# Talking-heads attention in a 12-layer decoder kernel: a third score buffer, another block order, and other places for the maxima

## The reference, cut to what matters

```python
dots = jnp.einsum('bhid,bhjd->bhij', q, k) * QK_SCALE
dots = jnp.einsum('hg,bgij->bhij', W_pre_th, dots)
dots = jnp.where(causal[None, None], mask_value, dots)     # column > row is masked
top = jax.lax.top_k(dots, TOPK)[0]                         # TOPK = 64
dots = jnp.where(dots < top[..., -1:], mask_value, dots)
attn = jax.nn.softmax(dots, axis=-1)
attn = jnp.einsum('hg,bgij->bhij', W_post_th, attn)
out = jnp.einsum('bhij,bhjd->bhid', attn, v) * head_scale_params
out = out.transpose(0, 2, 1, 3).reshape(b, n, H * DH) * jax.nn.sigmoid(x @ Wg + bg)
return out @ Wo                                            # then residual and layer norm
```

## Time and profile before

| what | us |
|---|---|
| median of 3 executions (lowest, highest) | 1305.36 (1302.91, 1308.99) |
| the profiled execution: its own time | 1304.4 |
| the span of its instructions | 1302.6 |
| DVE busy in the span | 969.4 (74%) |
| PE busy | 892.4 (69%) |
| ACT busy | 640.1 (49%) |

### The profile page before, as it was taken

How to read it: one execution, slowest core, us unless ns; L and a number is a source line. 1 busy time by engine, 2 the same in 40 slices (tenths; PEclk the granted TensorE clock), 3 DMA queues, 4 the chain that set the end, 5 groups by cost and what they waited for, 6 DMA issues and landing times. The chain is left out here.

```text
span 1302.6 us, 18521 instructions
## 1 busy us (share of the span) xinstructions
PE 892.4 (69%) x6150; PEld 590.5 (45%) x6150; DVE 969.4 (74%) x2494; ACT 640.1 (49%) x1416; POOL 245.0 (19%) x369
## 2 busy tenths in 40 slices
PE   5957676565875304245997939889978615999876
PEld 3533334333544203134884514667645304666644
DVE  5899999937663798987356855888868497898832
ACT  3767878712442405046315713787447411666632
POOL 1330000001000000000012220299522022332100
PEclk9985555566997657577998968899979767999978
DMA  6000000002456001011100000000000000000000
GB/s 213 2 2 0 1 1 1 1 1 97 106 125 133 5 1 67 1 67 34 34 1 1 2 1 1 1 1 1 2 1 1 1 0 0 2 2 2 2 1 17
DMA packets 26607, 30.12 MB, mean 23 GB/s; under 512 B 1169, under 2 KB 23057, under 8 KB 25490
## 3 DMA queue, kind: packets, MB, share of 16 engines
q1 hardware_dynamic: 26514, 28.95, 8.0%
HBM read 19.50 MB, written 9.44 MB: 22 GB/s over the span
## 5 line engine op out<-in xcount | busy, mean ns | idle before, releaser
L1986 PEld LDWEIGHTS l2a_b_ps<-l2a_diag,l2a_uT 128*128 128x128 f32 x512 | 66.1, 197 | 27.9 <-issue 15.4
L1986 PE MATMUL l2a_b_ps<-l2a_diag,l2a_uT 128*128 128x128 f32 x512 | 70.6, 283 | 4.7 <-DVE l2a_convh L2197 3.7
L2683 PE MATMUL l1w_mem_ps<-l1a_rows,l1w_post 128*128 128x64 f32 x16 | 4.6, 381 | 96.5 <-DVE l1a_rows L2825 96.5
L2798 DVE MATCH_REPLACE8 l1w_minus<-l1w_low,l1w_minus 128x129 f32<-128x129 f32 (+39 forms) x264 | 65.2, 298 | 0.0
L2711 ACT ACTIVATE l1w_score<-l1w_mix_ps 128x264 f32<-128x264 f32 (+7 forms) x29 | 12.1, 451 | 107.4 <-DVE l1a_rows L2825 91.4
L2792 DVE MAX8 l1w_low<-l1w_minus 128x8 f32<-128x129 f32 (+37 forms) x332 | 60.4, 291 | 0.4
L2673 PE MATMUL l1w_mix_ps<-l1a_rows,l1w_pre 128*128 128x264 f32 (+7 forms) x58 | 29.4, 677 | 43.0 <-DMA l1a_rows<-scores_dram 25.4
L2656 POOL TENSOR_SCALAR_AFFINE_SELECT l1w_score<-l1w_score 128x256 f32<-128x256 f32 x8 | 4.1, 506 | 246.7 <-ACT l1w_score L2711 246.7
L2683 PEld LDWEIGHTS l1w_mem_ps<-l1a_rows,l1w_post 128*128 128x128 f32 x16 | 4.0, 288 | 100.8 <-DVE l1a_rows L2825 99.7
L613 ACT ACTIVATE l3a_l3x_probT<-l3a_l3x_turn_ps 128x512 f32<-128x512 f32 x64 | 38.2, 596 | 22.7 <-PE l3a_l3x_turn_ps L494 21.9
L494 PE MATMUL l3a_l3x_turn_ps<-pack,l3a_l3x_prob 128*128 128x128 f32 x256 | 40.7, 282 | 10.3 <-ACT l3a_l3x_probT L613 5.7
(11 more groups left out here) (580 smaller groups left out, 2822.7 us busy)
## 6 DMA issues: line engine op xcount, KB each, us to landing
scores_dram<-l1p_dots SPq DMA_DIRECT2D x8, 924.0 KB, 7.1
l1a_rows<-scores_dram SPq DMA_DIRECT2D x5, 1056.0 KB, 5.0
l1a_rows<-scores_dram SPq DMA_DIRECT2D x24, 132.0 KB, 3.6
scores_dram<-l1p_dots SPq DMA_DIRECT2D x8, 132.0 KB, 3.7
pack<-in_pack SPq DMA_DIRECT2D x1, 761.5 KB, 9.7
pack<-in_pack SPq DMA_DIRECT2D x2, 321.5 KB, 6.6
pack<-in_pack SPq DMA_DIRECT2D x1, 612.0 KB, 11.6
pack<-in_pack SPq DMA_DIRECT2D x1, 576.0 KB, 10.6
```

The source lines that it names most:

```text
L1986: mm = nc.tensor.matmul(bx_ps(n)[:, j * S:(j + 1) * S], uT[:, c, b, :], diag[:, s % 2, b, :], start=True, stop=True)
L2798: nc.vector.match_replace(out=neg[:, i, 0:keys[i]], in_to_replace=low[:, i, :], in_values=neg[:, i, 0:keys[i]], imm_value=LOWEST).then_inc ...
```

## The change

- `ORDER_K` is 7, 0, 6, 1, 5, 4, 3, 2.
- There are three score areas: `score_a` for blocks k=7, 5, 3, `score_b` for 6 and 4, and `cm.taps` for 0, 1, 2. `copy_mixed` waits only for the last block that was in the same area (`held_last`). `low` lies behind the scores in `cm.taps`, and `neg_max` and `total` have three places.
- TensorE and ScalarE work two blocks ahead: `mix(n+2)` behind `mix_again(n-1)`, `copy_mixed(n+2)` behind `copy_again(n-1)`.
- The maxima stand in other places (`MAX_AFTER`): of the second block after round 0 of the first; of n=3 after round 2 of n=2; of n=5 after round 2 of n=4; of n=6 after round 0 of n=5; of n=7 after the weights of n=5; of n=2 and n=4 at the start of the unsearched block ahead of them, as before.
- In the first block the negation and the searches of round 0 are done per half block, as soon as that half's scores are copied, and `maximum(0)` follows them. GpSimd's mask of the first block waits for both negations.
- As `cm.taps` is now used in the weights stage, the taps are loaded at the start of `mixed_output`, and `dve_weigh` stands in VectorE's stream there, in the turn b = 4.

```diff
-ORDER_K = (7, 0, 6, 1, 5, 2, 4, 3)
+ORDER_K = (7, 0, 6, 1, 5, 4, 3, 2)
+MAX_AFTER = {(0, 0): 1, (2, 2): 3, (4, 2): 5, (5, 0): 6}
...
-                sp.dma_start(cm.taps, cm.A["l2a_taps"]).then_inc(cm.taps_loaded, 16)
...
-                tap_weights.dve_weigh(nc, dve, cm)
...
+        held = {7: score_a[:], 5: score_a[:], 3: score_a[:], 6: score_b[:], 4: score_b[:], 0: cm.taps, 1: cm.taps, 2: cm.taps}
+        score = [held[k] for k in ORDER_K]
+        held_last = {1: 0, 2: 1, 5: 7, 4: 6, 3: 5}
...
                     pool.wait_ge(mix_set, filled[n + 1])
+                    if n == 0:
+                        pool.wait_ge(minus_set, 2)
...
                 mix(0)
+                mix(1)
                 for n in range(BLOCKS_K + 1):
-                    if n + 1 < BLOCKS_K:
-                        mix(n + 1)
                     if n:
                         mix_again(n - 1)
+                    if n + 2 < BLOCKS_K:
+                        mix(n + 2)
...
                 def copy_mixed(n):
-                    if n >= 2:
-                        act.wait_ge(weights_set, n - 1)
+                    if k in held_last:
+                        act.wait_ge(weights_set, ORDER_K.index(held_last[k]) + 1)
...
                 copy_mixed(0)
+                copy_mixed(1)
                 for n in range(BLOCKS_K + 1):
                     if n < BLOCKS_K:
                         exponentials(n)
-                    if n + 1 < BLOCKS_K:
-                        copy_mixed(n + 1)
                     if n:
                         copy_again(n - 1)
+                    if n + 2 < BLOCKS_K:
+                        copy_mixed(n + 2)
...
-                maximum(0)
                 for n, k in enumerate(ORDER_K):
...
+                        def negate(first, last):
+                            nc.vector.tensor_scalar(neg[:, first:last, :], s[:, first:last, :], -1.0, None,
+                                                    ALU.mult).then_inc(minus_set, 1)
+                        if n:
+                            dve.wait_ge(kth, n_kth)
+                            negate(cut[0], ROWS_K)
...
                             for i in cut:
+                                if n == 0 and r == 0 and i % (ROWS_K // 2) == 0:
+                                    dve.wait_ge(mix_set, filled[1] * (i + ROWS_K // 2) // ROWS_K)
+                                    negate(i, i + ROWS_K // 2)
+                                    n_minus += 1
+                                    dve.wait_ge(minus_set, n_minus)
...
+                            if n == 0 and r == 0:
+                                maximum(0)
...
-                            if r == 0 and n + 1 < BLOCKS_K:
-                                maximum(n + 1)
+                            if (n, r) in MAX_AFTER:
+                                maximum(MAX_AFTER[n, r])
...
                     nc.vector.tensor_tensor(e, e,
+                                            bcast_last(total[:, n % 3, :], w), ALU.mult).then_inc(weights_set, 1)
+                    if n == 5:
+                        maximum(7)
...
 def mixed_output(nc, cm, mixed, v_all, ahead):
+            def _(sp):
+                sp.dma_start(cm.taps, cm.A["l2a_taps"]).then_inc(cm.taps_loaded, 16)
...
                         bias(b + 1)
+                    if b == B // 2:
+                        tap_weights.dve_weigh(nc, dve, cm)
```

More of the change, by code:

```diff
@@ L2602, in mixed_weights @@
         pre, post = sc.sb("pre", [128, 128]), sc.sb("post", [128, 128])
-        score = [sc.sb(f"score{odd}", [128, ROWS_K * max(block_width(k) for k in ORDER_K[odd::2])])
-                 for odd in range(2)]
+        score_a, score_b = (sc.sb(n, [128, ROWS_K * block_width(k)]) for n, k in (("score_a", 7), ("score_b", 6)))
+        held = {7: score_a[:], 5: score_a[:], 3: score_a[:], 6: score_b[:], 4: score_b[:], 0: cm.taps, 1: cm.taps, 2: cm.taps}
+        score = [held[k] for k in ORDER_K]
+        held_last = {1: 0, 2: 1, 5: 7, 4: 6, 3: 5}
         blocks, loaded_rows, rows_count = ahead.blocks, ahead.loaded_rows, ahead.rows_count
         minus = sc.sb("minus", [128, ROWS_K * J])
-        low = sc.sb("low", [128, ROWS_K, 8])
-        neg_max, total = sc.sb("neg_max", [128, 2, ROWS_K]), sc.sb("total", [128, 2, ROWS_K])
+        low = cm.taps[:, ROWS_K * block_width(2):ROWS_K * block_width(2) + ROWS_K * 8].rearrange("p (i e) -> p i e", e=8)
+        neg_max, total = sc.sb("neg_max", [128, 3, ROWS_K]), sc.sb("total", [128, 3, ROWS_K])
         mem_w = sc.sb("mem_w", [128, MEM, S])
@@ L2654, in _ @@
                     pool.wait_ge(mix_set, filled[n + 1])
-                    part = block_of(score[n % 2], k)[:, :, w - ROWS_K:]
+                    if n == 0:
+                        pool.wait_ge(minus_set, 2)
+                    part = block_of(score[n], k)[:, :, w - ROWS_K:]
                     pool.affine_select(out=part, in_=part, compare_op=ALU.is_ge, fill=LOWEST, base=0,
@@ L2710, in copy_mixed @@
                         act.wait_ge(mix_mm, u + 1)
-                        nc.scalar.activation(score[n % 2][:, f * m * w:(f + 1) * m * w], mix_ps[u % 4][:, 0:m * w],
+                        nc.scalar.activation(score[n][:, f * m * w:(f + 1) * m * w], mix_ps[u % 4][:, 0:m * w],
                                              ACT.Copy).then_inc(mix_set, 1)
@@ L2718, in exponentials @@
                     w = block_width(k)
-                    s, e = block_of(score[n % 2], k), blocks[n % ROW_BUFS][:, :, 0:w]
+                    s, e = block_of(score[n], k), blocks[n % ROW_BUFS][:, :, 0:w]
                     for i in range(ROWS_K):
-                        last = nc.scalar.activation(e[:, i, :], s[:, i, :], ACT.Exp, bias=neg_max[:, n % 2, i:i + 1],
-                                                    accum_out=total[:, n % 2, i:i + 1])
+                        last = nc.scalar.activation(e[:, i, :], s[:, i, :], ACT.Exp, bias=neg_max[:, n % 3, i:i + 1],
+                                                    accum_out=total[:, n % 3, i:i + 1])
                     last.then_inc(exp_set, 1)
@@ L2836, in mixed_output @@
         ln = LayerNorm(sc)
+        tap_weights = TapWeights(sc)
         wg, wo, mem_v, mem_w = ahead.wg, ahead.wo, ahead.mem_v, ahead.mem_w
@@ L2843, in mixed_output @@
         with nc.Block() as block:
+            @block.sync
+            def _(sp):
+                sp.dma_start(cm.taps, cm.A["l2a_taps"]).then_inc(cm.taps_loaded, 16)
             @block.gpsimd
```

29 lines of the change are left out of this document (11 added, 18 removed).

## The result

The changed kernel took 1298.23 us, median of 6 executions (1296.81 to 1300.70), against 1304.07 (1302.90 to 1308.99, 6 executions) of the kernel before on the same chip. The medians differ by 5.8 us. The ratio that is given with a run is not the quotient of the two medians. Here it is 0.9945, interval [0.9924, 0.9965]: 7.2 us faster, between 4.6 and 9.9. The prediction was 1299.9. Of the twelve executions when the changed kernel ran for the third time, one took 2125.20 us; it counts as disturbed and is left out of the ratios.

The account below looks back on a forecast made before the run. No engine is full over the whole span; the weights stage decides, with a VectorE part and a 7.0 us TensorE/ScalarE tail. Profiled 1304.4 less 5.5 is 1298.9, plus 1.0 for the median gives 1299.9; range 1295.5 to 1305.

Parts of the forecast that it names:

- The start: First block of the weights stage: VectorE's searches begin at 428.2, first strike-out at 435.2 instead of 438.0; gain 2.7 us.
- The middle: Weights stage up to block k=5: waits ahead of maxima go, weights of k=5 at 576.7, 11.5 us earlier.
- What is late next: Stage's end, last load (k=2) held behind ScalarE's exponentials: three new waits, some 6 of 11.5 us gained go back.
- The tail: Copies-out ending the weights stage: last copy at 620.4, before 625.80, gain 5.4 us; output stage's products start 5.5 earlier.
- The taps: Scores stage gain 0 (at most 0.3 us); output stage: 1.23 us of weighing hidden, load's cost taken as 0.
- Warm tail: Rival, stage's end: TensorE's groups at the high clock (0.9) from 584; gain 8 us, median 1297.3; chance 0.20.
- Tail takes all back: Rival, stage's end: TensorE's groups stay at 1.7 us; gain 0.6 us, median 1304.8; chance 0.12.
- Taps in the way: Rival, output stage's start: taps' load holds up `mem_w` by up to 6.5 us; at full price 1306.4; chance 0.06.
- A wait stays: Rival, middle: a maximum still waits for a late load, each wait giving back 1 to 3 us; 1302; chance 0.07.

## Why the prediction was right

*The start.* Predicted: searches from 428.2, 435.2 at the first strike-out, gain 2.7. The trace: work from 427.98, and the maximum with its negation done at 432.52 + 2.33 + 0.17, that is 435.0. Its copies were 0.2 ahead, so this is what was forecast. Undoing it cost 3.5 us in time and 1.8 to 3.2 in the stage's length. Shown.

*The middle.* Predicted: no wait ahead of five maxima, and the weights of k=5 at 576.7. They were done at 576.07, without a wait. Of what makes this so, the third area (without it 10.7 us slower) and the later places of the maxima (without them 10.0 to 11.4 us more stage) are both needed in the two-ahead order, where both were tried. The prediction put the area's worth into the waits ahead of the maxima of k=6 and k=5, about 5 us; taking the area away cost twice that in the changed order, because the same wait also holds exponentials. With the area neither wait exists, so this does not show in the sum.

*Two blocks ahead* had no term of its own in the prediction, and rightly: one ahead was no slower.

*What is late next.* Predicted waits of 4.8, 2.3 and 6 to 7 ahead of the last three steps of VectorE; the trace has 4.00, 2.39 and 7.36. Predicted mechanism: ScalarE's exponentials hold the copies-out, these hold TensorE at its second PSUM bank and the last load. The experiment with the exponentials moved took away 4.00 and 2.39 and 5 of the 7.36 us, and the one with more banks took TensorE's wait for a bank there from 3.59 to 1.08. So of 12.1 us gained by 576 some 6 went back in the queue order of one engine; two edits, which together made the stage 10 to 12 us shorter, show it.

*The tail.* Last copy predicted at 620.4, found at 620.21; first product of the output stage 623.4, found 623.20. That these agree to 0.2 us is partly luck. Up to the last block the trace runs ahead of the forecast: the weights of k=5 are 0.6 early, TensorE ends their remixing at 584.45 + 3.06 = 587.51, not 588.6, and the load is there at 592.39, not 593.9, which is 1.5 early. Then the copies-out take it back. That of k=4 took 606.27 - 601.34 = 4.9 and that of k=3 615.99 - 611.30 = 4.7, not the 4.0 that I had put down for each as a mean of both clocks: their last groups came 1.71 us apart, the low clock's pace. These two terms were 1.6 too small together, and the terms ahead of them about as much too large.

The prediction took the low pace of the groups of k=5 from the rest of 4 to 5 us ahead of them. The pace was so, but the clock had not fallen in that rest, as the last section shows.

*The taps.* Predicted at nothing, hidden; the trace agrees for the scores stage (a wait of 1.56 in place of 0.32 and the 1.23 of work), for the weighing in the output stage (0.96 of waiting left of 2.23) and for the load beside `mem_w` (a wait of 0.66, before 0.80). This rests on the trace of the changed kernel and was not undone by an experiment.

*The rivals.* Warm tail: fell, as the groups of the three copies-out ran for the most part at the low clock. Its own terms, 1.6 and twice 0.8, lead to 617.2 and not to its 617.7, but nothing hangs on this. Tail takes all back: fell, since the last block's groups ran at the high clock. Taps in the way: fell. A wait stays: fell. The predicted 1299.9 is 1.7 us above the measured median. Of this, 1.3 lies in its starting point: it took 5.5 us off the 1305.36 of three executions, and all six have a median of 1304.07. The stage's gain was as forecast: 5.4 us in the profile of the result, 6.1 and 4.7 in the two later ones. The ratios say some 7 us for the whole kernel; whether the difference to 5.5 is more than the spread of whole executions stays open.

## What to carry to other kernels

When a buffer is added so that one engine doesn't wait, look next at the order inside the in-order queue of the engine that serves it: here half of the gain went back because a copy that had to wait stood ahead of exponentials that were ready, and these, done late, stood ahead of copies that free PSUM banks and a row buffer. Turning that queue's last entries round gave 5.6 us, beside the 7.7 of the whole change in the same set of runs, and cost no memory. A wait that is removed can come back at the next place: in the two-ahead order the third area without later places for the maxima made the kernel slower than before. A wait in front of an instruction is paid by all that is queued behind it: price it by them, not by its own user.

## What was not expected of the hardware

TensorE's clock changed several times near the end of the stage, and not when the engine's work stopped or began. These are windows of the changed kernel: three rests of TensorE, each followed by the groups behind it, and the last block's groups. The columns are length, busy us of TensorE, its weight loads, VectorE, ScalarE, GpSimd, then granted clock, DMA share, GB/s. A granted clock of 0.50 is 1.2 GHz, 1.00 is 2.4 GHz.

```profile
580.20:584.40 4.20, 0.00 (x0) 0.00 (x0) 4.17 (x27) 4.20 (x25) 0.00 (x0) 1.00 0.00 0
585.50:587.50 2.00, 2.00 (x10) 1.71 (x9) 1.93 (x14) 0.60 (x1) 0.00 (x0) 0.50 0.00 0
597.70:602.00 4.30, 0.00 (x0) 0.00 (x0) 1.74 (x13) 4.30 (x26) 0.00 (x0) 1.00 0.00 0
602.50:605.50 3.00, 3.00 (x16) 3.00 (x16) 1.53 (x2) 0.60 (x1) 0.00 (x0) 0.50 0.00 0
607.80:612.00 4.20, 0.00 (x0) 0.00 (x0) 0.54 (x2) 4.20 (x26) 0.00 (x0) 1.00 0.00 0
613.00:615.50 2.50, 2.50 (x14) 2.50 (x13) 0.00 (x0) 0.71 (x2) 0.00 (x0) 0.50 0.00 0
616.00:620.00 4.00, 3.57 (x31) 3.38 (x30) 0.00 (x0) 2.28 (x5) 0.00 (x0) 1.00 0.49 148
```

In all three rests the granted clock stayed at 1.00, and it fell to 0.50 only after TensorE had begun again, within 1 us. So most of the two groups behind each rest ran at the low clock, 1.7 us from the one to the other, and the last block's groups came 0.9 apart. In a longer rest of the kernel before, the 8.2 us from 606.9 to 615.1, the clock did fall within the rest: it was 1.00 until 609 and 0.50 from 609.5 on.

The version with early exponentials and more banks shows a fourth case. There TensorE's last run of groups began at 593.32 behind a rest of 2.63 us, and the clock was 0.50 from 586 on, before and in that rest; it stayed at 0.50 until 598 and was 0.85 in the window behind:

```profile
594.00:598.00 4.00, 4.00 (x21) 4.00 (x21) 2.62 (x18) 4.00 (x26) 0.00 (x0) 0.50 0.00 0
598.00:602.00 4.00, 3.29 (x24) 3.10 (x23) 1.46 (x2) 4.00 (x26) 0.00 (x0) 0.85 0.00 0
```

There the low clock costs little, as ScalarE is busy for 4.00 of 4.00 us in both windows.
